# Attention with a routed expert layer: one turn moved ahead of a step's second product set, one moved between value products, and one copy split around an exponential

## The reference

```python
qkv = x @ qkv_w.T + qkv_b                      # x: (32, 256, 128)
q, k, v = jnp.split(qkv, 3, axis=-1)           # 16 heads of 8
att = jnp.einsum('bhqd,bhkd->bhqk', q, k) / np.sqrt(HEAD_DIM)
att = jax.nn.softmax(jnp.where(causal, att, -jnp.inf), axis=-1)
out = jnp.einsum('bhqk,bhkd->bhqd', att, v)
x = layernorm(x + out @ out_w.T + out_b)
x = layernorm(x + experts(x))                  # top 2 of 8
```

## Time and profile before

| | us |
|---|---|
| median of 3 runs | 982.62 (981.38 to 983.6) |
| the profiled execution's own time | 989.87 |
| its span in the trace | 988.1 |
| PE busy in the span | 799.6 (81%) |
| DVE busy | 585.2 (59%) |
| POOL busy | 552.4 (56%) |
| ACT busy | 480.5 (49%) |

### The profile page before, as it was taken

The page is one execution under the profiler, slowest core; times in us unless marked ns, Lnnn a source line. Parts: engine busy times, 40 slices in busy tenths (PEclk is TensorE's granted clock), DMA queues, the critical chain, the costliest instruction groups (busy, mean ns, idle before and its releaser), DMA issues. The chain is left out here.

```text
span 988.1 us, 22538 instructions
## 1 busy us (share of the span) xinstructions
PE 799.6 (81%) x7657; PEld 598.8 (61%) x7658; DVE 585.2 (59%) x1478; ACT 480.5 (49%) x1150; POOL 552.4 (56%) x719
## 2 busy tenths in 40 slices
PE   5899999999999999982538877888777778787866
PEld 3556666666666666551228776877767777686722
DVE  4678888888888888827935433434434343343445
ACT  1377777777777777755713222222223222222347
POOL 6146666666666666654054666656665656666543
PEclk9899999999999999975668988898998898999979
DMA  5334444434434443204921111111111111112178
GB/s 168 103 122 134 135 135 134 132 131 129 127 127 136 135 135 129 75 8 176 163 46 30 44 41 44 41 41 42 44 43 39 43 42 43 43 42 43 36 238 280
DMA packets 71596, 93.98 MB, mean 95 GB/s; under 512 B 10336, under 2 KB 50016, under 8 KB 71232
## 3 DMA queue, kind: packets, MB, share of 16 engines
q1 hardware_dynamic: 62640, 74.21, 24.1%
q0 software_dynamic: 8704, 17.98, 7.0%
q10 hardware_dynamic: 144, 0.35, 0.1%
HBM read 56.26 MB, written 34.14 MB: 91 GB/s over the span
## 5 line engine op out<-in xcount | busy, mean ns | idle before, releaser
L377 DVE TENSOR_REDUCE neg_max<-ps_s 128x6 f32<-128x768 f32 x256 | 241.1, 952 | 38.7 <-PE ps_s L564 32.7
L242 POOL TENSOR_SCALAR_AFFINE_SELECT probs<-probs 128x512 f32<-128x512 f32 x256 | 162.4, 634 | 164.7 <-ACT probs L314 159.1
L314 ACT ACTIVATE probs<-ps_st 128x768 f32<-128x768 f32 x256 | 207.5, 811 | 81.5 <-PE ps_st L578 80.9
L1122 ACT ACTIVATE act_a<-ps_a 128x352 f32<-128x352 f32 x136 | 63.5, 467 | 310.7 <-DMA dense<-shift_t 160.4
L1103 POOL DMA_INDIRECT picked_rows<-rows_out,pairs x136 | 134.0, 986 | 134.1 <-ACT rows_out L1126 109.9
L1096 POOL DMA_INDIRECT xg<-x_rows,pairs x136 | 131.6, 968 | 79.8 <-issue 40.5
L1160 DVE TENSOR_TENSOR x_low<-ps_xy,x_high 128x128 fp32r<-128x128 f32 x136 | 39.1, 287 | 216.6 <-ACT x_high L1130 173.6
L558 PE MATMUL ps_s<-dense 32*128 32x256 f32 (+1 forms) x1024 | 117.9, 306 | 19.1 <-ACT probs L314 9.3
L1231 PE MATMUL ps_xy<-w_sb,h_t 128*128 (+1 forms) x816 | 129.2, 300 | 1.7 <-ACT rows_out L1126 1.7
L558 PEld LDWEIGHTS ps_s<-dense 32*128 32x128 f32 x1024 | 82.2, 191 | 78.2 <-issue 46.7
L1231 PEld LDWEIGHTS ps_xy<-w_sb,h_t 128*128 128x128 f32 (+1 forms) x816 | 120.6, 213 | 7.1 <-issue 6.8
(11 more groups left out here) (181 smaller groups left out, 1390.6 us busy)
## 6 DMA issues: line engine op xcount, KB each, us to landing
dense_rows<-split SPq DMA_DIRECT2D x32, 512.0 KB, 2.7
dense<-dense_rows SPq DMA_DIRECT2D x64, 256.0 KB
dense<-dense_rows SPq DMA_DIRECT2D x64, 128.0 KB
pick<-picked_rows SPq DMA_DIRECT2D x16, 512.0 KB, 6.0
x_rows<-y_all SPq DMA_DIRECT2D x8, 520.0 KB, 8.1
xt_sb<-xt SPq DMA_DIRECT2D x32, 128.0 KB, 2.2
x_sb<-x SPq DMA_DIRECT2D x32, 128.0 KB, 2.4
out<-normal SPq DMA_DIRECT2D x16, 256.0 KB
```

The lines of the kernel that those rows point to most:

```text
L242: last = pool.affine_select(out=part, in_=part, compare_op=ALU.is_ge, fill=0.0, base=0, pattern=[[0, 2 * BLOCKS], [1, P]], channel_multipl ...
L314: act.activation(probs[:, g, 2 * half:2 * half + 2, 0:L + P], ps_st[:, :, 0:L + P], ACT.Exp, scale=float(HEAD_DIM) ** -0.5).then_inc(exp_d ...
L377: v.tensor_reduce(out=neg_max[:, h * GROUP + j:h * GROUP + j + 2, :], in_=ps_s[:, j:j + 2, 0:L + P].rearrange("p b (c t) -> p b c t", t=P) ...
```

## The change

Three edits, all in the lists of the attention.

1. **The split's copy in two.** ACT copies the queries' high part after both exponentials of step 0, and the keys' high part between the two exponentials of step 1. Each copy signals; DVE waits for the second.
2. **The shift's turn ahead of step 2's second set.** PE turns the parts of the maxima right behind the heads' turn, before product set (2, 1) instead of after its mask products. ACT copies the shift before exponential (2, 1) instead of after it.
3. **The mixed rows' turn between value products.** In step 3 PE turns the mixed rows after the second set's mask products and before the second set of value products, instead of after them. ACT copies the mixed rows before `out_t` instead of after it.

```diff
-            def take_split(b):
-                wait(act, split_made, b)
-                wait_landed(act, rows_written, b - 1)
-                for w, s in enumerate((Q_HIGH, K_HIGH)):
-                    last = act.activation(split[:, s, :], ps_m[:, w * L:(w + 1) * L], ACT.Identity,
-                                          bias=bqk_sb[:, w:w + 1])
-                last.then_inc(high_ready, 1)
+            def take_split(b, w):
+                if w == 0:
+                    wait(act, split_made, b)
+                    wait_landed(act, rows_written, b - 1)
+                act.activation(split[:, (Q_HIGH, K_HIGH)[w], :], ps_m[:, w * L:(w + 1) * L], ACT.Identity,
+                               bias=bqk_sb[:, w:w + 1]).then_inc(high_ready, 1)
...
                     if has(b):
                         exponentials(b, g, 0)
+                    if g == 1 and has(b + 3):
+                        take_split(b + 3, 1)
                     if g == 2 and has(b - 1):
                         take_heads(b - 1)
+                    if g == 2 and has(b + 1):
+                        take_shift(b + 1)
                     if has(b):
                         exponentials(b, g, 1)
-                    if g == 2 and has(b + 1):
-                        take_shift(b + 1)
                     if g == 0 and has(b + 3):
-                        take_split(b + 3)
+                        take_split(b + 3, 0)
...
+                    if g == 3 and has(b - 1):
+                        take_mixed(b - 1)
                     if g == 3 and has(b):
                         take_out(b, 0)
-                    if g == 3 and has(b - 1):
-                        take_mixed(b - 1)
...
             def take_low(b):
-                wait(dve, high_ready, b)
+                wait(dve, high_ready, b, 2, 1)
...
                     if g == 2 and has(b - 1):
                         turn_heads(b - 1)
+                    if g == 2 and has(b + 1):
+                        turn_shift(b + 1)
                     if g == 3 and has(b):
                         weighted(b, 0, 0)
                     products(b, g, 1)
                     if scored:
                         causal(1)
-                    if g == 2 and has(b + 1):
-                        turn_shift(b + 1)
...
+                    if g == 3 and has(b - 1):
+                        turn_mixed(b - 1)
                     if g == 3 and has(b):
                         weighted(b, 0, 1)
-                    if g == 3 and has(b - 1):
-                        turn_mixed(b - 1)
```

## The result

The changed kernel takes 970.58 us (median of 4 runs, 968.66 to 974.09) against 983.01 (median of 4) for the kernel before beside it: ratio 0.9885, 95% interval 0.9856 to 0.9914, so 12.4 us or 1.15% faster.

A forecast was written before the change was run, and what follows sets the result against it. Attention was taken as a 12.60 us ring of eight product sets, paced by the exponential's loop, PE's work and two long intervals. Gains of 0.04 + 0.03 + 0.03 a turn, times 30, gave 982.6 - 3.0 = 979.6 us; range 974.5 to 984.6.

The forecast's parts named there:

- Edit 1, 0.29 a turn: Interval from set (1, 0) to (1, 1): exponential starts 0.34 earlier, PE's own work then decides, 1.79 becomes 1.50, gaining 0.29.
- of the gain of 0.29 thus 0.04 a turn is left: Before set (2, 1): PE waits for DVE's parts, so the set starts at 209.59 to 209.60 instead of 209.64.
- the wait that the forecast had at 0.24: PE before set (2, 1): held by DVE's parts until 209.59, where the exponential would have allowed 209.35.
- The prediction's own two ends: Bounds at set (2, 1): 0.29 gained if DVE were early enough, 0.10 lost if the second copy comes 0.14 later.
- Edit 3, 0.03 a turn: Last interval of the turn, 1.86: POOL's `heads` decides; 0.03 gained, bounds 0.20 gained or 0.06 lost.
- The projection, 0.03 a turn: First set of the next turn: projection no longer waits for ACT, 1.49 falls to 1.45 or 1.46, gaining 0.03.
- The sum: Whole turn of the attention: 0.04 + 0.03 + 0.03 = 0.10 us gained, times 30 is 3.0 us.
- The one in which the parts are early and the change of form is saved in full: Shift's and mixed rows' turns: neither wait costs, 0.29 + 0.20 + 0.03 a turn, 15.6 us, 967.0; part of a rival, chance 0.10.
- The slower rival: ACT between exponentials (1, 0) and (1, 1): second copy late, low parts at 206.90 would give 987.4 us; chance 0.17.

The follow-up runs named there:

- the fill: Useless 128 x 128 fill on DVE ahead of the parts of the maxima: added to the changed kernel, ratio 0.9936; added to the kernel before, 0.9989.
- the last group: Last three kernels run beside the kernel before (898.4 us); among them the changed kernel again, unaltered: 888.56 us, ratio 0.9884.
- the best kernel found: Changed kernel with the shift's turn back in its old place and POOL's heads' product ahead of the residual's bias: ratio 0.983, then 0.9843 (884.86 us).

## Why the prediction was wrong, by its own steps

**Edit 1, 0.29 a turn: right.** The exponential follows its set by 0.49 and the interval is 1.49, as forecast; edit 1 alone gives 0.30 a turn.

**Edit 2, "of the gain of 0.29 thus 0.04 a turn is left": this is the step that failed.** The mechanism is there: PE waits for DVE's parts, and lateness passes through one for one. The size of the wait was wrong. Counted from set (1, 0), the forecast had the parts end at 4.21 and set (2, 1) start at 4.69; measured are 4.11 (205.06 - 200.95) and 4.50. Three small terms were too long, all the same way. The low parts start 1.70 behind the set, not 1.74: the second copy ends where it was forecast (1.67 behind the set, 1.66 forecast), but DVE's wake is 0.03 (202.62 to 202.65), and the 0.08 taken for it is read from a row of POOL, not of DVE. From the last reduction's start to the parts' end it is 1.62, not the 1.68 copied from the earlier trace rows. There the reduction began 0.05 behind the low parts' end, here 0.09 ahead of it, and nearly all of the difference is in the first small instruction behind it, 0.24 long there and 0.18 here; it is 0.24 in every kernel without edit 1 and without the fill, 0.18 in every one with edit 1 and without the fill, and no run shows why. And from the parts' end to the set it is 0.39 (205.06 to 205.45), not 0.48: the shift's two weight loads, 0.21 long before where they follow other work, take 0.11 where they have waited (210.14 and 205.12 above), while the wake (0.06 for 0.07) and the idle time ahead of the set's load (0.21 for 0.20) were right. Together they are 0.19, and the wait that the forecast had at 0.24 is one of 0.06. It is the difference of two chains that run side by side, and three links of one of them were off by 0.04 to 0.09. The prediction's own two ends, 0.29 gained and 0.10 lost, did hold the result; its central value was put where the errors added up, and the range of the time was made narrower than those ends.

**Edit 3, 0.03 a turn, between 0.20 gained and 0.06 lost: mechanism right, size nearly.** Measured 0.06 (medians 1.863 to 1.805), with PE waiting for `heads`. That `choice` moves up by 0.13 because of edit 2, and that without this the edit loses 0.06, both came out (0.07 lost in two runs). The full saving with no wait is 0.15 (1.86 to 1.71), not 0.20. The Trainium skill's rule that a change of tiling mode drains TensorE (TensorEngine Tiling (Array Packing), Key Properties) gave the direction, and these runs bear it out: 0.15 for one change less. Not every change of form in the rows has this price, though: the shift's turn is one from 128x128 to 128x32, and its loads stand idle 0.5 us in 20 turns.

**The projection, 0.03 a turn: right**, 1.48 to 1.45, also in edit 3 alone. `out_t` fits in front of the exponential.

**The sum.** 0.10 a turn was forecast and 0.32 measured: 0.19 to 0.20 from the wait for the parts and 0.03 from edit 3. Over 31 turns 0.32 is 9.9 us; the two traces have 9.6 in them. The timed difference is 12.4 with an interval from 8.5 to 14.2, which holds the 9.9; what there is beyond the turns was not traced to anything, and in the last group the medians of the same two kernels differ by 9.8.

**The rivals.** The one in which the parts are early and the change of form is saved in full had half of its condition: 967.0 was given for it, nearer to the result than the forecast was. Its two halves together are the best kernel found, 0.48 a turn instead of its 0.52. The slower rival was decided at low parts 0.10 later than forecast; they were 0.04 earlier.

## What to carry to other kernels

When a gain is passed into a wait for another engine, what is left of it is the difference of two chains, and errors of 0.05 us in links are as large as the answer: take each link from a row of the same engine in which it did wait and start at once, and where none exists give the whole width to the range. A turn moved ahead into a place where its input is just due can pay by what it clears on a third engine (here ACT's logits, then POOL's `heads`); ask whether that engine's own order does it without the wait. Undoing each edit singly and reading the intervals of one turn, not the total, tells 0.06 us apart where the timing of whole runs does not.

## What the runs showed of the hardware

- A fill of 0.165 us in front of three small DVE instructions delayed the last of them by 0.07 us only in the changed kernel, and by 0.02 in the kernel before; the first of them is 0.24 us long in the turn of the earlier trace rows, 0.18 in the changed kernel and 0.12 behind the fill in both. This would fit if part of such an instruction's time were one of waiting for what stands before, in which another instruction can lie; no run shows it apart from this.
- Putting two pieces of full-array TensorE work side by side saved one change of form: 0.15 us of 1.86, where the idle time in front of a load behind such a change is 0.20.
- The same two weight loads are 0.21 us long together where they follow other work and 0.11 behind a wait for DVE (medians over the turns of the kernel before and of the changed one).
- The same changed kernel took 970.6 us in the first measurement and 888.6 in the last. A different chip is not shown to be the reason: the kernel before took 989.3 us in one group and 898.4 in another, and both groups bear the same chip number. The last exponential starts at 430.1 us in the one trace and 433.1 in the other, so the whole difference lies behind the attention. There, from 450 to 880 us, GpSimd stands idle far more in front of its gathers in the first. The groups of the first, with 117 of its 136 gathers in that stretch, and then of the second, with all of them (busy us, mean ns, idle before and what ended it):

```profile
L1104 POOL DMA_INDIRECT picked_rows<-rows_out,pairs x117 | 115.5, 987 | 108.8 <-ACT rows_out L1127 87.7 <-issue 21.1
```

```profile
L1104 POOL DMA_INDIRECT picked_rows<-rows_out,pairs x136 | 134.1, 986 | 44.2 <-issue 37.2 <-ACT rows_out L1127 7.0
```

  One instruction of them is equally long in both (987 and 986 ns). The granted clock differs less than the time does: 0.88, 0.89 and 0.91 in the three stretches of 100 us from 500 to 800 us in the first, 0.93, 0.95 and 0.92 in the second. Why the expert part is slower in the first stays open.
